# A selective scan and a feed-forward block: B's product, the sum over states and the gate in another form

## What is computed

```python
# first part: x = x + xattn(ctx, z = layernorm(x)); per batch, channels e (256), states n (16), time l (256)
h     = in_proj_w @ ctx^T                    # 256 channels
u     = silu(causal_conv4(h) + conv_b)
dt_lo, Bm, Cm = split(x_proj_w @ u)          # 8, 16 and 16 rows
delta = softplus(dt_proj_w @ dt_lo + dt_proj_b)
state = state * exp(delta * A[e, n]) + (delta * u) * Bm[n]     # over time
y     = sum_n state[e, n] * Cm[n] + D * u
x     = x + (y * silu(z))^T
# second part: x = x + ffn(layernorm(x)), with rounded activations and ternary weights
gate, val = silu(bit_linear(x, gate_w, gate_b)), bit_linear(x, val_w, val_b)
x = x + bit_linear(gate * val, out_w, out_b)
```

## Time and profile before

| | us |
|---|---|
| median of 3 runs | 228.26 |
| lowest, highest | 226.56, 228.98 |
| span of the profiled execution (first to last instruction) | 224.8 |

### The profile page before, as it was taken

How to read it: one execution, slowest core, us unless ns; L and a number is a source line. 1 busy time by engine, 2 the same in 40 slices (tenths; PEclk the granted TensorE clock), 3 DMA queues, 4 the chain that set the end, 5 groups by cost and what they waited for, 6 DMA issues and landing times.

```text
span 224.8 us, 2405 instructions
## 1 busy us (share of the span) xinstructions
PE 150.9 (67%) x706; PEld 92.9 (41%) x706; DVE 186.5 (83%) x284; ACT 129.3 (58%) x197; POOL 136.8 (61%) x132
## 2 busy tenths in 40 slices
PE   6983088643979197059630777926986667899983
PEld 5531054232636186048620533504435265334552
DVE  3789999998089999999999968797869998838661
ACT  2578675336585996076341758736498015376772
POOL 5036499778900999896685999999139202691000
PEclk9995559978585769758785596985589969999999
DMA  4894943261400223004003304314000000000002
GB/s 107 231 343 123 339 146 112 87 189 42 140 13 0 75 66 92 4 0 141 0 0 98 135 3 136 73 71 140 23 1 3 23 0 0 0 28 0 23 23 70
DMA packets 12689, 17.44 MB, mean 78 GB/s; under 512 B 3468, under 2 KB 9012, under 8 KB 12678
## 3 DMA queue, kind: packets, MB, share of 16 engines
q1 hardware_dynamic: 12678, 17.30, 24.5%
HBM read 16.11 MB, written 1.19 MB: 77 GB/s over the span
## 4 chain that ended last, share of the span: by engine, by line
DVE 19%; PE 16%; ACT 9%; issue 6%; POOL 5%; DVEq 0%; POOLq 0%; ACTq 0%
DVE wstate L908 3%; PE work L1242 2%; DVE state L898 2%; PE work L1282 2%; DVE gam L981 2%; DVE xhat L825 2%; PE decay L1067 2%; ACT decay L653 2%; DVE pool_state L898 2%; DVE wstage L976 2%; POOL drive L491 2%; ACT gT L722 2%; ACT wstage L703 1%; PE decay L1242 1%; PE work L1249 1%
## 5 line engine op out<-in xcount | busy, mean ns | idle before, releaser
L491 POOL TENSOR_TENSOR drive<-du,b_wide 128x1024 f32<-128x1024 f32 x31 | 74.2, 2407 | 2.9 <-DVE state L898 1.8
L653 ACT ACTIVATE decay<-delta,aneg 128x510 f32<-128x510 f32 x64 | 42.9, 684 | 45.9 <-DVE state L898 23.3
L898 DVE TENSOR_TENSOR_SCAN state<-decay,drive 128x512 f32<-128x512 f32 x44 | 52.4, 1208 | 0.9 <-issue 0.9
L1156 PE MATMUL ysum<-ident,wstate 128*128 128x128 f32 x176 | 32.9, 332 | 10.6 <-DVE wstate L908 10.6
L908 DVE TENSOR_TENSOR wstate<-state,cwide 128x512 f32<-128x512 f32 x44 | 29.1, 663 | 12.2 <-issue 11.8
L1156 PEld LDWEIGHTS ysum<-ident,wstate 128*128 128x128 f32 x176 | 26.1, 172 | 18.8 <-DVE wstate L908 13.8
L501 POOL TENSOR_TENSOR pool_wstate<-pool_state,c_wide 128x1024 f32<-128x1024 f32 x10 | 23.7, 2367 | 11.4 <-PE ysum L1156 8.6
L898 DVE TENSOR_TENSOR_SCAN pool_state<-decay,drive 128x512 f32<-128x512 f32 x20 | 24.3, 1214 | 0.2 <-ACT decay L653 0.2
L1067 PE MATMUL work<-ident,wstage 128*128 128x128 f32 x80 | 14.2, 331 | 11.4 <-ACT ternary L677 7.7
L1177 PE MATMUL cwide<-cparts,sel 128*128 128x512 bf16 x22 | 10.6, 483 | 15.4 <-DVE wstate L908 14.2
L1067 PEld LDWEIGHTS work<-ident,wstage 128*128 128x128 f32 x80 | 11.8, 174 | 12.7 <-ACT ternary L677 8.1
(11 more groups left out here) (180 smaller groups left out, 298.7 us busy)
## 6 DMA issues: line engine op xcount, KB each, us to landing
b_wide<-bc_rows SPq DMA_DIRECT2D x16, 512.0 KB, 4.5
c_wide<-bc_rows SPq DMA_DIRECT2D x10, 256.0 KB, 3.5
x_in<-in_x SPq DMA_DIRECT2D x2, 512.0 KB, 4.9
wstage<-in_L_ffn_gate_w SPq DMA_DIRECT2D x1, 1024.0 KB, 7.8
wstage<-in_L_ffn_val_w SPq DMA_DIRECT2D x1, 1024.0 KB, 10.3
wstage<-in_L_ffn_out_w SPq DMA_DIRECT2D x1, 1024.0 KB, 9.0
ctx_in<-in_ctx SPq DMA_DIRECT2D x2, 256.0 KB, 4.4
out<-wtap SPq DMA_DIRECT2D x4, 128.0 KB, 1.7
```

The source lines that it names most:

```text
L491: nc.gpsimd.tensor_tensor(drive[:, m % NDR], du[:, m // NS], rows.unsqueeze(1).to_broadcast([P, EH, W]), ALU.mult).then_inc(s_drive, 1)
L653: nc.scalar.activation(v[:, :, 1:L], d[:, :, 1:L], ACT.Exp, scale=aneg[:, eh, n:n + 1]).then_inc(s_decay, 1)
L898: nc.vector.tensor_tensor_scan(dst, decay[i % ND][:], drive[:, i // EH % NDR, i % EH], 0.0, ALU.mult, ALU.add).then_inc(s_scan, 1)
L1156: last = nc.tensor.matmul(ysum[:, k, eh * P:(eh + 1) * P], lhsT=src[:, k * P:(k + 1) * P], rhs=ident[:], start=start and k % LB == 0, stop ...
```

## The change

The two sides share the feed-forward part nearly word for word. Changed are:

1. **Layout of a slot.** The loop still has 64 units, but a unit is now one batch of a group and a *pair* p of states, for one half eh; two units (the two batches) make a slot. There are 32 slots. A tile is [2 batches, 2 states, 256 steps]; the scan runs over 2 states x 256 steps of one batch. Decays are in SBUF (four slots deep), du*B in four PSUM banks.
2. **du*B on TensorE** (`drives`). du is turned once per group and half (`turn_du`); GpSimd writes diagonal matrices of B's values (`diagonals`, an affine select of 128x1024 per pair), and a matmul of turned du with two diagonals gives du*B for 128 steps and two states. `drives(i+3)` is issued at step i, `sums` of a slot five steps behind.
3. **Weighing with C on GpSimd** for 31 of 32 slots (`weigh`, 128x1024), the last one on VectorE. C's rows come by DMA for all slots.
4. **Sums with the identity standing** (`sums`): y keeps channels on the partitions. The skip term is a matmul of u with a diagonal of D.
5. **The gate**: silu((x - m)*r) by ScalarE (`silu_x`) without turning x; y is gated, then turned (`turn_y`), then x is added.
6. **Softplus**: relu on VectorE, and the four terms are added by TensorE (`add_delta`); dt_proj and x_proj's first rows are folded into one weight `wdT` at the start, so pre comes straight from u.
7. The ternary weights come out of Sign on ScalarE (no clipping on VectorE); one scaling instruction less per scale; other loop tables.

Cut from the diff:

```diff
-PE_PRE, ACT_PRE = (13, 14), (16, 18)
+PE_PRE, DVE_RELU, ACT_SOFT = (11, 11), (12, 13), (13, 15)
+DVE_SLOTS = (NSLOT - 1,)
+DRIVE_LEAD = 3
+SUM_LAG = 5
...
-        decay = [pb(f"decay{i}", [P, BANK]) for i in range(ND)]
-        cwide = pb("cwide", [P, BANK])
-        ysum = pb("ysum", [P, GT, DI])
+        ysum = pb("ysum", [P, EH, BANK])
+        drive = [pb(f"drive{i}", [P, BANK]) for i in range(NDRV)]
...
-                    nc.gpsimd.tensor_tensor(drive[:, m % NDR], du[:, m // NS],
-                                            rows.unsqueeze(1).to_broadcast([P, EH, W]), ALU.mult).then_inc(s_drive, 1)
+            def diagonals(k):
...
+                nc.gpsimd.affine_select(out=bdiag[:, k % NDG].rearrange("p t n l -> p (t n) l"),
+                                        in_=values.unsqueeze(2).to_broadcast([P, GT * 2, P]),
+                                        compare_op=ALU.is_equal, fill=0.0, base=0, pattern=[[0, GT * 2], [-1, P]],
+                                        channel_multiplier=1).then_inc(s_diag, 1)
...
+            def weigh(s):
...
+                pool.wait_ge(s_scan, BG * s + BG)
+                pool.wait_ge(s_cload[k % NCW], 16 * (k // NCW + 1))
+                if r >= NPW:
+                    pool.wait_ge(s_ysum, s - NPW + 1)
+                flat = lambda v: v.rearrange("p b n l -> p (b n l)")
+                nc.gpsimd.tensor_tensor(flat(pool_wstate[:, r % NPW]), flat(state[:, s % NST]), flat(c_wide[:, k % NCW]),
+                                        ALU.mult).then_inc(s_poolw, 1)
...
+            def silu_x():
...
+                for t in range(B * LB):
+                    nc.scalar.activation(xs[:, t], x_in[:, t], ACT.Silu, bias=nv[:, 2, t:t + 1],
+                                         scale=nv[:, 1, t:t + 1]).then_inc(s_xs, 1)
...
             t = wait_full(act, "dtw")
             release(nc.scalar.activation(dtwT[:], t[0:DR, 0:EH * P].rearrange("p (h e) -> p h e", h=EH), ACT.Copy), "dtw")
+            t = wait_full(act, "wd")
+            release(nc.scalar.activation(wdT[:].rearrange("p h e -> p (h e)"), t[:], ACT.Copy), "wd")
...
+            for i in range(ACT_QUANT[-1] + ACT_LEAD + 1):
+                if i < NUNIT:
+                    decays(i)
+                if i == 3:
+                    copy_delta(0, 1)
+                    turned_du(0, 1)
+                    taps(1)
+                t = i - ACT_LEAD
...
-            def add_to_y(src, g, eh, start):
-
-                for k in range(GT):
-                    last = nc.tensor.matmul(ysum[:, k, eh * P:(eh + 1) * P], lhsT=src[:, k * P:(k + 1) * P],
-                                            rhs=ident[:], start=start and k % LB == 0, stop=True,
-                                            is_transpose=True, skip_group_check=True)
-                return last
+            def add_delta(g, eh):
...
+                nc.tensor.matmul(t[:], lhsT=ident[:], rhs=relu[:, eh], start=True, stop=False)
...
+                nc.tensor.matmul(t[:], lhsT=ident[:], rhs=mag[:, eh], start=False, stop=False)
...
+                nc.tensor.matmul(t[:], lhsT=nident[:], rhs=back[:, eh], start=False, stop=False)
...
+                fill(nc.tensor.matmul(t[:], lhsT=ident[:], rhs=lnw[:, eh], start=False, stop=True), name)
...
+            def drives(i):
...
+                if i >= NDRV:
+                    pe.wait_ge(s_scan, i - NDRV + 1)
...
+                pe.wait_ge(s_diag, k + 1)
+                bank = drive[i % NDRV][:].rearrange("p (n l) -> p n l", n=2)
+                for c in range(LB):
+                    t = b * LB + c
+                    last = nc.tensor.matmul(bank[:, :, c * P:(c + 1) * P], lhsT=duT[:, g, t, eh], rhs=bdiag[:, k % NDG, t],
+                                            start=True, stop=True)
+                last.then_inc(s_drive, 1)
+
+            def sums(s):
...
+                for n in range(2):
+                    last = nc.tensor.matmul(ysum[:, eh], lhsT=ident[:], rhs=src[:, :, n], start=False, stop=True,
+                                            skip_group_check=True)
+                last.then_inc(s_ysum, 1)
...
+            for name in ("bt0", "wd", "xc00", "conv1"):
+                wait_read(pe, name)
+            for i in range(DRIVE_LEAD):
+                drives(i)
...
             for i in range(PE_OUT[-1] + 1):
-                scan_step(i)
+                if i + DRIVE_LEAD < NUNIT:
+                    drives(i + DRIVE_LEAD)
+                if i >= SUM_LAG and (i - SUM_LAG) % BG == 0:
+                    s = (i - SUM_LAG) // BG
+                    if s < NSLOT - 1:
+                        if s == SLOTS:
+                            skips(1)
+                        sums(s)
```

More of the change, by code:

```diff
@@ L69 @@
[L69 to L86, removed]
@@ L89, in sums_at @@
[L89 to L95, removed]
+NP = NS // 2
+SLOTS = NP * EH
+UNITS = SLOTS * BG
+ORDER = [(0, 0), (1, 0), (0, 1), (1, 1)] + [(p, eh) for p in range(2, NP) for eh in range(EH)]
+NSLOT = G * SLOTS
+NUNIT = G * UNITS
+ND = 4
+NDRV = 4
+NST = 3
+NPW = 2
+NDG = 3
+NCW = 3
+DVE_SLOTS = (NSLOT - 1,)
@@ L133, in work_tiles, with place @@
     tiles, used = {}, [0] * 8
-    for names, banks in ((first, (0, 1, 2, 3)), (scans, (0, 1)), (last, (4, 5, 6, 7, 0, 1))):
+    def place(name, bank):
+        tiles[name] = (bank, used[bank])
+        used[bank] += 1
+    for name, bank in first.items():
+        place(name, bank)
+    for names, banks in ((scans, (0, 1)), (last, (4, 5, 6, 7, 0, 1))):
         for i, name in enumerate(names):
-            bank = banks[i % len(banks)]
-            tiles[name] = (bank, used[bank])
-            used[bank] += 1
+            place(name, banks[i % len(banks)])
     return tiles
@@ L1001, in _ @@
+            make_du(0, 0)
+            release(nc.vector.tensor_copy(delta[:, 0, 0], wait_full(dve, "dl00")[:]), "dl00")
+            rounded(0, 1)
+            t = wait_full(dve, "dut00")
+            release(nc.vector.tensor_copy(duT[:, 0, :, 0], t[:].rearrange("p (t e) -> p t e", t=GT)), "dut00")
+            make_du(0, 1)
+            for i in range(NUNIT):
                 scan(i)
-                if i and not on_pool(i - 1):
-                    weigh(i - 1)
+                if i % BG == BG - 1 and i // BG in DVE_SLOTS:
+                    weigh(i // BG)
@@ L1122, in convolve_tap, with pre_delta @@
                     fill(last, name)
+            def pre_delta(g, eh):
+                name = f"pre{g}{eh}"
+                t = work_tile(name)
+                if g == 0:
+                    wait_read(pe, "wd")
+                for k in (1, 0):
+                    wait_u(pe, g, k)
+                    last = nc.tensor.matmul(t[:], lhsT=wdT[:, k, eh * P:(eh + 1) * P], rhs=u[:, k], start=k == 1,
+                                            stop=k == 0)
+                fill(last, name)
             def project(g):
-                name = f"proj{g}"
+                name = f"bc{g}"
                 t = work_tile(name)
@@ L1180, in sum_step @@
[L1180 to L1192 removed]
+                    wait_u(pe, g, eh)
```

871 lines of the change are left out of this document (420 added, 451 removed).

## The result

| | before | after |
|---|---|---|
| median of 4 runs each, us | 227.79 (226.56 to 228.98) | 243.46 (241.60 to 244.66) |
| span of the profiled execution, us | 224.8 | 242.9 |
| time of that execution, us | not on record | 244.66 |

The ratio is 1.073, with a 95% interval of 1.064 to 1.081: slower by 15.7 us. The forecast was 243.5 us.

The account below looks back on a forecast made before the run. TensorE was taken to bound the scan stage: 31.1 us start, 162.7 work, 6 stalls, 3 clock give 202.8; with 37.2 of tail the span is 240.0, plus 3.5 makes 243.5 us. Range 232 to 268 us, slower at 0.90.

Parts of the forecast that it names:

- The price of an fp32 product: On TensorE: an fp32 matmul of 512 columns is two records of 0.43 us, 0.86 us together at full clock.
- The upper bound of 59: du*B on TensorE: up to 59 us if each change of weights costs extra; 55.0 without, 56.5 taken.
- The stage: First du*B to last sum: 162.7 us of TensorE work at full clock, plus 6 for stalls and 3 for clock.
- Stalls and clock: Scan stage: 6 us of TensorE stalls, 3 us for two half-speed stretches, otherwise clock 1.00 with a full queue.
- The one stall that I placed: Scan stage, steps 38 and 41: VectorE's burst of some 18 us against 14 of TensorE, a stall of 4 us.
- The rivals at 0.75 and 0.87: Scan-stage TensorE clock: staying at 0.75 gives 295 us, chance 7%; half that sag, 0.87, gives 268 us, 13%.
- bound 108.5: VectorE in the scan stage: upper bound of 108.5 us of work, keeping all its other work, so below TensorE's.
- The rival of full relief: Scan stage: TensorE keeps up and VectorE bounds with 122 us; 194.5 us in total, faster; chance 5%.
- The start: Ahead of the scans: first du*B at 31.1 us, first scan about 32.1, 5.2 us later than 26.94.
- six matmuls, 5.2 us, to 19.6: In the start: TensorE takes up pre and B/C at 14.4 us, six matmuls in 5.2 us, ending at 19.6.
- The tail: From the last sum to the end: left at 37.2 us, TensorE bounding there.
- The sum: Whole kernel: sums end at 202.8 us, span 240.0, plus 3.5 us from span to unprofiled median, 243.5 us.

Follow-up runs that it names:

- the first four experiments: Single edits of the changed kernel: sums by turns 226.48 us, bf16 du*B 220.14, every second slot weighed by VectorE 245.87, u made before the weight copy 243.22.
- giving back the sums: Changed kernel with slots summed by transposes with the identity streamed, as before, instead of matmuls with the identity standing; 226.48 us, 1.004 of before.
- turned sums: Changed kernel with sums by transposes and u made before the folded weight's copy: 224.76 us with softplus added on TensorE, 229.07 us with it on VectorE.
- u first: Changed kernel with ScalarE making both halves of u ahead of the copy of the folded weight; 243.22 us.
- the 211.93 us: Changed kernel with sums by transposes, du*B from bf16, and u made before the folded weight's copy; 211.93 us, 0.939 of before.
- delta on VectorE: Changed kernel with softplus's four terms added by VectorE in SBUF instead of by fp32 matmuls on TensorE; 246.68 us.
- delta on VectorE and idle turns: Kernel with softplus added on VectorE, plus 68 unread identity turns filling TensorE's waits in the start; 245.01 us over four executions.

## Why the prediction was right, by its own steps

- **The price of an fp32 product** (two records, 0.86 us per 512 columns) held at all its new uses, and carries the result. Sums: 32 x 1.72 = 55.0 us, as predicted. Drives: 64 x 0.865 = 55.4, predicted 56.5. The upper bound of 59, a charge for each change of weights, was not needed, and its own row gives less: eight at 0.11 us instead of 0.1075 make 55.0 into 56.3.
- **The stage** was to be 162.7 + 6 + 3 = 171.7 us from the first drive to the last sum; it was 171.35. TensorE's idle time in it is 6.2 us, where 6 was predicted; half clock cost the 1.6 us named below, where 3 was; which leaves 163.6 us of work, where 162.7 was. So here the terms are right and not only their sum.
- **Stalls and clock.** The one stall that I placed, after step 38 and 41, is there: 1.32 + 3.29 = 4.6 us against 4. The half clock behind it costs 1.0 us on the drives (2.07 against 1.03) and 0.6 on the sums (2.50 against 1.88), where I had taken 3 for two such stretches. A full queue kept the clock: 1.00 from 90 to 120 us with TensorE busy 30.00 of 30.00 us. The rivals at 0.75 and 0.87 fell. The time of the second, 268 us, contains the 3 us for clock, which the first leaves out; without them its terms give 265. The rule of the Trainium skill ("TensorE: Matmul & The Clock Gate", on the HAM clock gate) that was weighed there holds in this trace, 0.99 over the stage.
- **VectorE** did 104.87 us in the stage (bound 108.5) and waited for the drives. **GpSimd's diagonals** took 1.11 us each, predicted 1.1 between 0.29 and 2.3; its 95.94 us, with 100 predicted, lie off the path. The rival of full relief fell with the two records a product.
- **The start was short by 2.3 us**: first drive at 33.37 us, predicted 31.1; first scan 34.61, predicted 32.1. u came when I said (ScalarE's second half of it ends at 14.65, predicted 15.0). What failed is the step "six matmuls, 5.2 us, to 19.6": after its wait of 1.39 us TensorE ran at clock 0.68, pre took 5.37 us, and B/C ended at 21.4. In the batch of the first four experiments pre took 3.67 us and the first scan of the same order stood at 33.59, so of the first scan's 2.5 us 1.0 belongs to this one execution and 1.5 to my chain of small steps.
- **The tail** took 38.2 us, predicted 37.2. TensorE works there 30.76 us against 31.25 before, but behind a wait of 2.22 us the clock is 0.79 from 210 to 218 us, as this last row of the changed kernel shows; before, the clock was 1.00 throughout its tail.

```profile
210.00:218.00 8.00, 5.78 (x24) 2.34 (x23) 3.37 (x10) 2.87 (x7) 6.54 (x31) 0.79 0.05 16
```

- **The sum.** Span predicted 240.0, measured 242.9 in the profiled execution (2.3 of start, 1.0 of tail, less 0.4 of stage) and 239.8, 241.6 and 241.8 in the other three. Around the span I added 3.5 us, by setting before's median against the span of one execution. That term is wrong: time less span is 1.7 to 1.8 in all four executions of after, and in the later executions of before it is 2.0 to 2.4 with one at 3.2. So the hit to within 0.1 us is luck in its last 1.7 us: the median span was 1.7 above my 240.0, and the time around it 1.7 below my 3.5. The bound, the price of the products and the length of the stage are not luck; they came out one by one.
- **The gain that was meant** is there and lies off the path: VectorE's work in the stage fell from 141.26 to 104.87 us, and its scans now wait 25.5 us for drives. TensorE was recorded busy 102.30 of 159.30 us, but at a mean clock of 0.75, so the old work would be about 77 us at full clock, an estimate from these two numbers. It was given 55 us of drives, 25 more of sums and 7 for the second group's softplus, 87 in all: about 164, and 165.28 was measured. With 6.2 us idle that is the new stage.
- By parts: giving back the sums is worth 17.0 us, du*B in bf16 23.3 us (with another result). Softplus on VectorE costs 3.2 us alone and 4.3 with turned sums, probably with lost clock in it. Moving the weighings to GpSimd is worth some 2.4 us while TensorE sets the time. The later start, 7.7 us, was predicted at 5.2 and not taken apart beyond the 1 us of u first.
- Not settled: why the clock after a wait of 1.4 us is full in one execution and half in another, and what VectorE and ScalarE each hold of the 211.93 us.

## What to carry to other kernels

Count each engine's work after the change before you count what the old bound is relieved of: TensorE had 57 us idle in its stage, some 82 at full clock by the estimate above, and was given 87. For each product, read from the trace what its form costs on TensorE: the same sum was 0.87 us per slot as turns of fp32 and 1.72 as a product with the identity, and du*B 0.865 us a step in fp32 and 0.22 in bf16, without its lower bits. Look at the start by itself: 7.7 of the 18.1 us lie ahead of the first scan. And where the changed engine is nearly level with the others, time taken off it comes back in part as waits and lower clock (25.1 us less work gave 18.3 us less span, 41 us of cheaper products gave 24.3), most at bursts of another engine that are longer than its lead.

## What the hardware showed that I had not expected

- VectorE's 128x512 fp32 operations on two SBUF operands take 0.69 us alone and 1.46 to 2.74 beside GpSimd's weighings and selects, and end 0.5 us after GpSimd's; the 64 scans keep 1.21 us on the mean, with GpSimd as busy as ever (one of a scan's operands, the drive, stands in PSUM).
- TensorE's clock was lower behind short waits: behind one of 1.39 us it was 0.68 on the mean, behind 3.29 us a step's drives took 2.07 us instead of 1.03, and behind 2.22 us in the tail it was 0.79, and with delta on VectorE twelve drive records took 5.00 us behind one of 0.63 us that had others of 3.72 and 4.46 shortly ahead of it. In other executions the wait of 1.39 us left pre at 3.67 us, so the length of the wait alone does not decide. The kernel with delta on VectorE and idle turns took 241.5 to 242.6 us at a mean clock of 0.99 and 247.4 to 247.6 at 0.965.
